# Mixture of experts: every expert on every token, or the tokens sorted by expert on the chip

## What is computed

```python
x = L0_attn_x
xn = _layernorm(x, axis=-1)
s = _L0_attn_ref(xn, L0_attn_w_in, L0_attn_w_out)          # 16 heads, windows of 64 keys
g = _silu(_L0_ffn_ref(xn, gate_w, wg, wu, wd, swg, swu, swd))
#   softmax(xn @ gate_w.T) over 8 experts, the two largest kept and made to sum to 1 (w1, w2)
#   expert e:  (silu(xn @ wg[e]) * (xn @ wu[e])) @ wd[e]     wg, wu: 128 x 176, wd: 176 x 128
#   plus one shared expert of the same form with 352 inner features, for every token
x = x + s * g
...                                                         # the second layer, untouched
```

## Time and profile before

| what | value |
|---|---|
| median of 3 runs | 1713.17 us (1711.78 to 1713.24) |
| span of the profiled execution | 1708.8 us |
| busy over the span: PE, DVE, ACT, POOL | 89%, 77%, 71%, 64% |
| front | 0 to 30.8 us |
| first attention | 30.8 to 261.6 us |
| experts | 261.6 to 559.8 us |
| second layer | 559.8 us to the end |

### The profile page before, as it was taken

How to read it: one execution, slowest core, us unless ns; L and a number is a source line. 1 busy time by engine, 2 the same in 40 slices (tenths; PEclk the granted TensorE clock), 3 DMA queues, 4 the chain that set the end, 5 groups by cost and what they waited for, 6 DMA issues and landing times. The chain is left out here.

```text
span 1708.8 us, 44008 instructions
## 1 busy us (share of the span) xinstructions
PE 1513.5 (89%) x16988; PEld 1164.6 (68%) x16988; DVE 1319.0 (77%) x2187; ACT 1217.6 (71%) x2065; POOL 1099.4 (64%) x661
## 2 busy tenths in 40 slices
PE   5899996999999499999999578899999999999885
PEld 4677774677776266666666467777777777777774
DVE  5899974555655699999997788887888888888753
ACT  2677774545445488888888378888888888888873
POOL 1777752555555388888887477776676777667614
PEclk8899998999999699999999689999999999999997
DMA  5000000000000500000000001111111110111113
GB/s 174 2 3 3 3 3 15 15 8 7 7 7 1 185 2 2 14 2 14 2 14 11 13 22 31 27 26 27 27 27 27 27 26 22 26 27 27 27 27 105
DMA packets 56837, 44.12 MB, mean 26 GB/s; under 512 B 28152, under 2 KB 47900, under 8 KB 56388
## 3 DMA queue, kind: packets, MB, share of 16 engines
q1 hardware_dynamic: 56644, 41.45, 9.1%
HBM read 17.75 MB, written 4.23 MB: 13 GB/s over the span
## 5 line engine op out<-in xcount | busy, mean ns | idle before, releaser
L831 POOL TENSOR_TENSOR a_prob<-a_prob,a_top 128x1024 f32<-128x1024 f32 x128 | 239.8, 1895 | 48.2 <-DVE a_top L1023 48.2
L1237 POOL TENSOR_TENSOR e_hh<-e_h,e_hh 128x512 fp32r<-128x512 f32 x112 | 144.8, 1293 | 146.6 <-ACT e_hh L1221 145.2
L1506 POOL TENSOR_TENSOR i_qk<-i_qk,i_rt 128x1024 f32<-128x1024 f32 x64 | 152.0, 2375 | 38.1 <-DVE i_rt L1955 33.3
L1516 POOL TENSOR_TENSOR i_qk<-i_qk,i_rn 128x1024 f32<-128x1024 f32 x64 | 122.5, 1915 | 80.5 <-DVE i_rn L1934 80.5
L1019 DVE TENSOR_TENSOR a_prob<-ps,a_table 128x1024 f32<-128x1024 f32 x128 | 149.7, 1211 | 23.4 <-PE ps L899 21.3
L1811 ACT ACTIVATE i_prob<-i_prob,i_top 128x128 f32<-128x128 f32 x512 | 156.4, 391 | 15.7 <-DVE i_top L1943 13.8
L977 ACT ACTIVATE a_probT<-ps 128x1024 f32<-128x1024 f32 x128 | 131.3, 1026 | 44.5 <-PE ps L907 44.5
L1258 DVE TENSOR_TENSOR e_h<-ps,e_sg 128x512 f32<-128x512 f32 x112 | 77.3, 690 | 104.3 <-PE ps L1120 90.4
L907 PEld LDWEIGHTS ps<-ident,a_prob 128*128 128x128 f32 x1024 | 113.2, 141 | 64.2 <-ACT a_probT L977 50.3
L1503 POOL TENSOR_TENSOR i_qk<-i_raw,i_rot 128x1024 f32<-128x1024 f32 x59 | 140.3, 2378 | 24.1 <-issue 24.1
L1208 ACT ACTIVATE e_sg<-ps 128x512 f32<-128x512 f32 x112 | 67.0, 598 | 123.2 <-PE ps L1120 122.4
(11 more groups left out here) (305 smaller groups left out, 4369.3 us busy)
## 6 DMA issues: line engine op xcount, KB each, us to landing
i_V<-i_V SPq DMA_DIRECT2D x96, 130.0 KB, 2.3
a_table<-skew_scratch SPq DMA_DIRECT2D x2, 2048.0 KB, 12.4
X<-in_L_attn_x SPq DMA_DIRECT2D x4, 512.0 KB, 6.1
a_table<-in_c_l_table SPq DMA_DIRECT2D x1, 2048.0 KB, 8.3
e_xs<-Y SPq DMA_DIRECT2D x8, 256.0 KB, 2.3
i_ms<-Y SPq DMA_DIRECT2D x16, 128.0 KB, 2.4
i_ms<-Y SPq DMA_DIRECT2D x16, 112.0 KB, 2.4
out_dram<-X SPq DMA_DIRECT2D x7, 256.0 KB, 2.3
```

What stands on the lines that cost most here:

```text
L831: nc.gpsimd.tensor_tensor(s, s, top[:, slot].unsqueeze(2).broadcast_to([P, HG, KW]), ALU.subtract).then_inc(shifted, 1)
L1237: nc.gpsimd.tensor_tensor(hh[0:n, slot(b, parity), 1, :], h[0:n, slot(b, parity), :], hh[0:n, slot(b, parity), 0, :].bitcast(F32), ALU.sub ...
L1506: nc.gpsimd.tensor_tensor(s, s, rt[:], ALU.add).then_inc(rotated, 1)
L1516: nc.gpsimd.tensor_tensor(flat, flat, rn[:, T // TPB % 2, T % TPB].unsqueeze(2).broadcast_to([P, 2 * FH, FD]), ALU.mult).then_inc(qk_done, 1)
```

## The change

The experts stage is replaced by a sparse one, and three earlier stages do work for it.

- **Router.** `choose_experts` still picks two experts per token, but then numbers the 8192 pairs: a PE job `rank` in the attention (two fp32 products of 256 columns) counts, for each token, the earlier rows of its tile that chose the same expert; a scan over the 32 tiles on DVE (5 steps) adds the tiles before; the experts' counts are rounded up to whole tiles of 128 and scanned. The result is a destination row for each pair (`at`) and, for each of 72 slot tiles, the offset of its expert's weights (`weights_at`). All this is DVE work at steps 4, 8, 12 and 16 of the attention (before: 4, 12, 20, 28 and 36).
- **Front.** SP writes zeros over the 72 x 128 slot rows in DRAM (9 transfers of 512 KB, rows of 512 bytes), ahead of the experts' weights in its list, and waits for them before the stage ends. The weights are kept once, as fp32, an expert after the other.
- **Attention.** From unit 24 on POOL issues two indirect scatters after each unit's `shift`: each sends the 128 rows of one tile of Y to their rows in DRAM. There are 64, in units 24 to 55.
- **Experts, slot part.** 36 pairs of slot tiles. For each pair SP loads 256 sorted rows; PE loads two offsets into registers (`value_load`), transposes the rows, multiplies with the chosen expert's 352 columns in fp32 (a register holds the address), transposes the product of ACT's silu and DVE, and multiplies with `wd`; SP writes the 256 results to DRAM.
- **Experts, shared part.** When all results are stored, POOL issues 64 indirect gathers, two per tile. Beside them the 8 rounds of the shared expert run: 18 fp32r products, 4 transposes and 12 fp32 products of 128 columns each on PE, and on DVE `mix`, which waits for the round's 8 gathers.
- Semaphores of finished stages are cleared by SP and used again.

The diff, cut to its core:

```diff
@@ front, SP's list
             sp.dma_start(rel[:, :], t["L1_attn_rel_bias"]).then_inc(rel_loaded, 16)
+            sp.dma_start(route["rank"][:], t["c_rank"]).then_inc(route["loaded"], 16)
+            sp.dma_start(route["slots"][:, :], t["c_slots"]).then_inc(route["loaded"], 16)
+            sp.wait_ge(nothing_set, 1)
+            for a in range(0, SLOTS, 8):
+                g, b = divmod(a, GROUP_SLOTS)
+                sp.dma_start(plan["xp"][g][b * P:(b + 8) * P, :].rearrange("(c p) e -> p c e", p=P), nothing[:]).then_inc(plan["cleared"], 16)
...
             sp.dma_start(skew, ext[:, :]).then_inc(rel_out, 16)
             sp.wait_ge(rel_out, 16)
+            sp.wait_ge(plan["cleared"], 16 * SLOTS // 8)
@@ helper
+def scatter_rows(nc, Y, plan, n, c):
+    where = bass.IndirectOffsetOnAxis(ap=plan["at"][:, n, c:c + 1], axis=0)
+    nc.gpsimd.indirect_dma_start(out=plan["xp"][n // GT], out_offset=where, in_=Y[:, n, :], in_offset=None).then_inc(plan["scattered"][n // GT], 16)
@@ choose_experts, part 2 (tile scan)
+        while reach < GT:
+            src, dst = tile_scan[:, side], tile_scan[:, 1 - side]
+            nc.vector.tensor_tensor(dst[:, :, PAD:PAD + GT, :], src[:, :, PAD:PAD + GT, :], src[:, :, PAD - reach:PAD + GT - reach, :], ALU.add)
+            dve.drain()
+            reach, side = 2 * reach, 1 - side
@@ window_attention
+        RANK = 7
+        CHOICE = (4, 8, 12, 16)
+        SCATTER = 24
+        EACH = 1 if GROUPS > 1 else 2
...
                 shift(n)
-                i, r = divmod(n + 2, U)
+                if n == SCATTER:
+                    pool.wait_ge(plan["placed"], 1)
+                for m in range((n - SCATTER) * EACH, (n - SCATTER + 1) * EACH):
+                    if 0 <= m < 2 * GT:
+                        scatter_rows(nc, Y, plan, *divmod(m, 2))
@@ experts, SP
+            for j in range(PAIRS + LAG):
+                if is_pair(j):
+                    if j % GROUP_PAIRS == 0:
+                        sp.wait_ge(scattered[j // GROUP_PAIRS], 16 * 2 * GT)
+                    after(sp, xs_T, j - XB + 1)
+                    sp.dma_start(xs[:, j % XB], rows(xp, j)).then_inc(xs_loaded[j % XB], 16)
+                if is_pair(j - LAG):
+                    d = j - LAG
+                    sp.wait_ge(ys_sb, d + 1)
+                    sp.dma_start(rows(yp, d), ys[:, d % YB]).then_inc(ys_out[d % YB], 16)
@@ experts, POOL
+            for n in range(NT):
+                if n % GT == 0:
+                    results_stored(pool, (n // GT + 1) * GROUP_PAIRS)
+                for v in range(2):
+                    where = bass.IndirectOffsetOnAxis(ap=plan["at"][:, n, v:v + 1], axis=0)
+                    nc.gpsimd.indirect_dma_start(out=yg[:, n, v, :], out_offset=None, in_=yp[n // GT], in_offset=where).then_inc(gathered[n // 4], 16)
@@ experts, PE
+            def place_weights(j):
+                for k in range(2):
+                    t = 2 * j + k
+                    chosen[t] = nc.tensor.value_load(weights_at[0:1, t:t + 1], min_val=0, max_val=(NE - 1) * EW)
+            def first_products(j):
+                pe.wait_ge(xs_sb, j + 1)
+                after(pe, h_sb, j - 1)
+                for k in range(2):
+                    last = nc.tensor.matmul(ps[:, 2 * (j % 2) + k, 0:2 * INTER], xsT[:, j % 2, k * P:(k + 1) * P],
+                                            flat[:, bass.ds(chosen[2 * j + k], 2 * INTER)], start=True, stop=True)
+                last.then_inc(gu_ps, 1)
...
+            for step in STEPS:
+                if is_pair(step + 1):
+                    place_weights(step + 1)
+                if is_pair(step):
+                    first_products(step)
+                if is_pair(step - 1):
+                    slot_hidden(step - 1)
+                if is_pair(step + 2):
+                    slot_tokens(step + 2)
+                if is_pair(step - 2):
+                    slot_results(step - 2)
+            for i in range(ROUNDS + 1):
+                if i == 0:
+                    tokens(0)
+                if i < ROUNDS:
+                    shared_products(i)
+                if i + 1 < ROUNDS:
+                    tokens(i + 1)
+                if i:
+                    shared_results(i - 1)
@@ experts, DVE
+            def mix(i):
+                dve.wait_ge(gathered[i], 16 * 8)
+                dve.wait_ge(down, i + 1)
+                after(dve, x_new, i - 1)
+                for v in range(2):
+                    for k in range(4):
+                        n = 4 * i + k
+                        rest = upd[:, i % 2, k, :] if v else ps[:, 6, k * P:(k + 1) * P]
+                        last = nc.vector.scalar_tensor_tensor(upd[:, i % 2, k, :], yg[:, n, v, :], share[:, n, v:v + 1], rest, ALU.mult, ALU.add)
```

More of the change, by code:

```diff
@@ L233, in router_buffers @@
 def router_buffers(nc, ctx):
     sb = lambda n, s, d=F32: ctx.enter_context(nc.sbuf_tensor("r_" + n, s, d))
[L236 to L244, removed]
+    wide = {n: sb(n, [P, NT, NE]) for n in ("lg", "rest", "first", "second", "chosen", "place")}
@@ new lines, in choose_experts @@
+        dve.drain()
+    elif part == 3:
+        for k in range(3):
+            src, dst, reach = slot_scan[:, k % 2], slot_scan[:, 1 - k % 2], 1 << k
+            nc.vector.tensor_tensor(dst[:, :, EPAD:EPAD + NE], src[:, :, EPAD:EPAD + NE], src[:, :, EPAD - reach:EPAD + NE - reach], ALU.add)
+            dve.drain()
+        begin = slot_scan[:, 1, :, EPAD - 1:EPAD + NE - 1]
+        for g in range(GROUPS):
+            nc.vector.scalar_tensor_tensor(grouped(place)[:, g], begin[:, g].unsqueeze(1).broadcast_to([P, GT, NE]), float(P), grouped(place)[:, g], ALU.mult, ALU.add)
+        dve.drain()
+        for c, one in enumerate((first, second)):
+            nc.vector.tensor_tensor(rest[:], place[:], one[:], ALU.mult)
+            dve.drain()
+            nc.vector.tensor_reduce(where[:, :, c], rest[:], AX.X, ALU.add)
+            dve.drain()
+        nc.vector.tensor_copy(plan["at"][:], where[:]).then_inc(plan["placed"], 1)
+    else:
+        begin = slot_scan[0:1, 1, :, EPAD - 1:EPAD + NE - 1]
+        full = [1, GROUPS, GROUP_SLOTS, NE]
+        numbers = slots[:, :].rearrange("p (g t) -> p g t", g=GROUPS)
+        nc.vector.tensor_tensor(listing[:], numbers.unsqueeze(3).broadcast_to(full), begin.unsqueeze(2).broadcast_to(full), ALU.is_ge)
+        nc.vector.tensor_tensor(st[:, :], best[:, 0, :], best[:, 1, :], ALU.add)
+        dve.drain()
+        nc.vector.tensor_reduce(numbers, listing[:], AX.X, ALU.add)
@@ L284, in choose_experts, with front @@
         dve.drain()
[L285 to L299, removed]
+def front(nc, t, ps, X, Y, ident, wts, plan, skew, attn, route):
+    full = SHARED // P
@@ new lines, in shared_results @@
+            def shared_results(i):
+                if i == 0:
+                    pe.wait_ge(ys_sb, PAIRS)
+                pe.wait_ge(ht_sb, (i + 1) * NC)
+                after(pe, mixed, i)
+                for k in range(4):
+                    for s, (a, n) in enumerate(CH):
+                        last = nc.tensor.matmul(ps[:, 6, k * P:(k + 1) * P], h[0:n, i % 2, s, k * P:(k + 1) * P], swd[0:n, s, :],
+                                                start=s == 0, stop=s == NC - 1)
+                last.then_inc(down, 1)
@@ new lines, in new_rows @@
+            def new_rows(i):
+                dve.wait_ge(gated, i + 1)
+                here = slice(4 * i, 4 * i + 4)
+                nc.vector.tensor_tensor(upd[:, i % 2], upd[:, i % 2], S[:, here, :], ALU.mult)
+                dve.drain()
+                nc.vector.tensor_tensor(X[:, here, :], X[:, here, :], upd[:, i % 2], ALU.add).then_inc(x_new, 1)
+                dve.drain()
+                for k in range(4):
+                    nc.vector.bn_stats(stats[:, 4 * i + k, :], X[:, 4 * i + k, :])
@@ L1291, in inner_layers @@
+            for i in range(ROUNDS + 2):
+                if i < ROUNDS:
+                    for s in range(NC):
+                        products(i, s)
+                if i + 1 < ROUNDS:
+                    low_tokens(i + 1)
+                if 1 <= i <= ROUNDS:
+                    mix(i - 1)
+                if i >= 2:
+                    new_rows(i - 2)
+def inner_layers(nc, t, ps, ident, X, Y, kept, out, weights, stored):
     KW = 2 * WIN
```

506 lines of the change are left out of this document (271 added, 235 removed).

## The result

The changed kernel took 1718.28 us (median of 11 runs, 1715.92 to 1721.04) against 1713.24 (11 runs, 1708.57 to 1717.34): a ratio of 1.0032, 95% interval 1.002 to 1.0044. It is slower by 0.3%, little but clear of the noise. The forecast was 1704, faster. The profiled execution took 1717.28 with a span of 1715.4.

The account below looks back on a forecast made before the run. PE was taken to bound the experts stage, DVE and PE together the attention. Front +12, DVE +2, scatters +39.5 and experts -63 gave -9.5 us, so 1704 us; range 1650 to 1785.

Parts of the forecast that it names:

- The attention: DVE +2: In the attention, the new router's some 31 small DVE instructions replace some 26, at 0.43 us each: +2 us.
- p: Price of one 128-row indirect transfer on POOL, taken as 1.1 us; at 1.17 the change is worth nothing.
- the shared part: Experts stage after the slots: 64 gathers at 1.1 us plus landings and final arithmetic, 81 us.
- +43.5: Attention units 24 to 55: two scatters a unit make POOL's unit 4.57 us instead of 3.21, +43.5 us.
- -9.5: Whole span: the changes in front, attention and experts together were to shorten it by 9.5 us.
- The slots: Experts stage, slot part: 5 us opening plus 149 us for 36 pairs with filling and emptying, 154 us.
- The step of 4.0: Slot part: 4.0 us a pair, with PE's products at 3.1 and register loads and arithmetic on top.
- The third rival: Slot part: PE's sequencer bounds it at 5.5 us a pair, 54 us more, total 1758 us; chance 0.14.
- the front: Front: nine zero writes of 512 KB go ahead of the weights and SP waits for them, +12 us.
- the last units: End of the attention: the four units by which DVE is ahead absorb about 4 us of the scatters' cost.
- the rounds' own 73: Shared part: the eight rounds on PE and DVE alone would take 73 us and lie under the gathers.
- The first rival: Attention and gathers: POOL's transfers are dear, 1.4 us each, giving 1742 us in total; chance 0.27.

## Why the prediction was wrong

**One step that failed is "The attention: DVE +2".** It set 31 small instructions against 26 at 0.43 us each and took the difference of the totals. The count was wrong: between the units the old router has 19 instructions in the trace and the new one 35 (28 and 46 with the part ahead of the first unit). Where they lie was left out: up to the 25th shift the old router had two parts between units, 69.5 to 72.7 and 96.1 to 99.0 us, 6.1 us of DVE (the first instruction of each):

```profile
69.50 0.41 DVE L249 TENSOR_REDUCE r_st<-r_rest 128x32 f32<-128x256 f32 x1
...
96.07 1.22 DVE L275 TENSOR_TENSOR r_wdense<-r_lg,r_first 128x256 f32<-128x256 f32 x1
```

The new one has five there, 3.2 + 0.8 + 7.5 + 5.2 + 3.6 = 20.3 us, on an engine that the same text names as one of the two that bound. And the waits were left out: seven of the new instructions were 0.3 to 1.6 us longer than their kind, 6.9 us in all, each of them beside POOL's 1.90 us. The term measured +13.3; moving the later parts away gave 14.0 back.

**The other, and the larger, is p.** It was bounded by 0.43 and 1.9 and set at 1.1, "a little below the middle". It is 1.22 in the attention and 1.29 on the mean in the gathers. The text's own point of return, 1.17, lies between the guess and the measurement, so the sign hung on 0.1 us in a bracket of 1.5. In the attention this made +50.6 of +43.5, in the shared part 64 x 0.19 = 12 of the 12.8 that it was longer: 19 us together. The reason for the price was right: a fixed part, hardly any per row. Either step alone turns the sign of the forecast's -9.5.

**The slots went the other way.** The step of 4.0 was to be an array of 3.1 and 0.9 of registers. It is 3.5, all of it array: the products with `wd` cost more than the earlier trace rows, for a reason that stays open, the register loads nothing. 154 became 137.2. So it is partly luck that the time came out only 14 us above the forecast: terms that were 32 us too low met one that was 17 too high. The third rival and the skill's floor fall with it: the Trainium skill, DMA: Bandwidth & Descriptors, section on latency and other measured facts, gives `tensor_load` a floor of about 600 ns. The rows show 302 in the median and 576 at most, and the step is as long without them; they are issued a step ahead.

**Right:** the front (+13.2 for +12), though the runs show SP's issuing and the transfer engines one behind the other; the last units (-4.1 for -4); that POOL is full and late twice, with DVE's `mix` waiting for the gathers; the rounds' own 73.

Sum: -9.5 forecast; +1.2 in the front, +11.3 on DVE, +7.1 for the scatters, -0.1 in the last units, -16.8 for the slots, +12.8 behind them, +0.9 later, is +6.9, and the span grew by 6.6; the 0.3 is rounding. The first rival named the mechanism that took the gain, at a smaller price than its 1.4; that DVE's router would take as much again was in none of them.

## What to carry to other kernels

A transfer with indices cost POOL 1.2 to 1.3 us with 128 rows and still 1.24 with 64, so what counts is where POOL's queue can make someone wait. Cutting the work into two groups, so that one group's transfers lie beside the other's products, won 47 us here (1.0032 to 0.9755), 14 us of padding already paid. Work added to an engine that is full has to be priced instruction by instruction in the units where it lands, not as a difference of totals; and a place that is free in one version (step 40 while POOL was full) is not in the next. And a price that sits in a wide bracket, with the break-even inside, is no ground for a sign: forecast the break-even, and give both sides their share.

## What the runs showed of the hardware

- DVE and POOL: DVE instructions of 0.16 to 0.20 us took 0.96 to 2.28 when they met one of POOL's 1.90 us operations, and ended within 0.05 us of it; where two of POOL's stood back to back one took 3.78. Beside POOL's indirect transfers the instruction with two inputs took its usual 0.74, in the one place that was seen.
- In the other direction it is smaller: six of the 64 gathers took 1.29 to 1.32 us instead of 0.94, each of them beside DVE's product of two SBUF tensors (L1422) that had begun 0.2 us earlier; no other gather met that product. No run takes the product away.
- SP: 512 KB in 1024 rows took it 1.75 us to issue, in 128 rows 0.44; then a write landed 12.3 us after its issue instead of 6.6, and a later issue took 9.7.
- TensorE's mean granted clock was 0.83 to 0.90 of 2.4 GHz where PE had idle time behind POOL, and 1.0 in these units when the wait was gone; between 20 and 30 us in the front it was 0.50 (1.2 GHz), 0.79 and 0.92 in three executions with the same work, and at 0.50 the attention started 6 to 7 us later than in the others.
